# Two MLPs of a vision block: the up-products in five passes of 128 rows instead of six of 96

## The reference, cut to what matters

```python
xn2 = layernorm(x, ln2_g, ln2_b)                       # rows of 192 channels
h = gelu(xn2 @ mlp_w1 + mlp_b1, approximate=False)     # 192 -> 768
x = x + (h @ mlp_w2 + mlp_b2)                          # 768 -> 192
```

## Time and profile before

| | us |
|---|---|
| median of three runs | 1113.1 (1109.18 to 1114.78) |
| the profiled execution | 1113.89, span of its core 1112.1 |
| PE / DVE / ACT / POOL busy | 1031.7 / 848.8 / 700.5 / 169.4 |
| TensorE clock granted, mean | 0.958 |

### The profile page before, as it was taken

The page is one execution under the profiler, slowest core; times in us unless marked ns, Lnnn a source line. Parts: engine busy times, 40 slices in busy tenths (PEclk is TensorE's granted clock), DMA queues, the critical chain, the costliest instruction groups (busy, mean ns, idle before and its releaser), DMA issues.

```text
span 1112.1 us, 35970 instructions
## 1 busy us (share of the span) xinstructions
PE 1031.7 (93%) x15606; PEld 727.9 (65%) x15606; DVE 848.8 (76%) x1714; ACT 700.5 (63%) x1003; POOL 169.4 (15%) x142
## 2 busy tenths in 40 slices
PE   5876879899999999999999999999989888998998
PEld 3555145665777776677677767676657765775776
DVE  4856968899999999999999999999526765233443
ACT  4666056677777777777777877787865442231554
POOL 4430000910000000000000000000024543001443
PEclk9885579999999999999999999999999999999999
DMA  4698966657474757565656566554400011211110
GB/s 126 163 228 274 245 124 152 108 88 135 81 126 92 115 96 108 96 107 100 104 100 104 105 99 109 95 98 85 80 13 22 24 26 33 66 54 40 41 45 22
DMA packets 83043, 109.17 MB, mean 98 GB/s; under 512 B 14141, under 2 KB 75266, under 8 KB 82693
## 3 DMA queue, kind: packets, MB, share of 16 engines
q1 hardware_dynamic: 82885, 106.87, 48.8%
HBM read 85.40 MB, written 21.44 MB: 96 GB/s over the span
## 4 chain that ended last, share of the span: by engine, by line
PE 70%; DVE 13%; DMA 8%; ACT 4%; issue 3%; POOL 2%; SPq 0%; DVEq 0%; ACTq 0%
PE ps L1044 35%; PE ps L1204 17%; PE ps L1039 15%; DVE mx_p L1499 5%; DVE xh L101 2%; POOL rstd L109 1%; DMA m_d<-mneg 1%; DVE stats L88 1%; DMA rel_d<-stage_lo 1%; PE ps L1057 1%; DVE stage_lo L1468 1%; DMA qv<-m_d 1%; DMA rel<-in_c_rel_w 1%; ACT hid_f L971 1%; PE ps L1150 1%
## 5 line engine op out<-in xcount | busy, mean ns | idle before, releaser
L1499 DVE TENSOR_REDUCE mx_p<-ps 128x1 f32<-128x464 f32 (+1 forms) x1080 | 608.2, 627 | 37.2 <-PE ps L1044 27.5
L921 ACT ACTIVATE prob<-ps 128x768 f32<-128x768 f32 x648 | 495.8, 810 | 188.9 <-PE ps L1044 188.3
L1044 PE MATMUL ps<-kc,qc 112*32 112x464 f16 (+1 forms) x4320 | 462.1, 371 | 8.4 <-issue 4.7
L1044 PE MATMUL ps<-qv,ka 113*32 113x384 f16 x5184 | 405.2, 328 | 11.6 <-DMA qv<-m_d 9.2
L1204 PE MATMUL ps<-prob,v_ext 128*32 128x384 f32 x2592 | 294.6, 487 | 3.9 <-issue 3.4
L1044 PEld LDWEIGHTS ps<-qv,ka 113*32 113x32 f16 x5184 | 213.4, 97 | 88.7 <-issue 31.0
L1044 PEld LDWEIGHTS ps<-kc,qc 112*32 112x32 f16 x4320 | 173.4, 96 | 108.2 <-DVE mx_p L1499 29.4
L1204 PEld LDWEIGHTS ps<-prob,v_ext 128*32 128x32 f32 x2592 | 117.1, 111 | 20.1 <-issue 5.8
L1039 PE MATMUL ps<-w_dn,hid 128*96 128x192 f16 x864 | 76.1, 246 | 8.6 <-DVE hid L1554 6.3
L1039 PEld LDWEIGHTS ps<-w_dn,hid 128*96 128x96 f16 x864 | 71.7, 123 | 14.0 <-DVE hid L1554 7.3
L768 POOL COPY v_ext<-v_all 128x288 f32<-128x288 f32 x12 | 5.0, 426 | 479.7 <-PE ps L1204 479.6
(11 more groups left out here) (106 smaller groups left out, 837.2 us busy)
## 6 DMA issues: line engine op xcount, KB each, us to landing
qv<-rel_d SPq DMA_DIRECT2D x216, 144.0 KB
qv<-kq_d SPq DMA_DIRECT2D x108, 216.0 KB
qc<-rel_d SPq DMA_DIRECT2D x24, 216.0 KB, 4.0
xin<-in_x SPq DMA_DIRECT2D x12, 288.0 KB, 3.6
kq_d<-khl SPq DMA_DIRECT2D x24, 144.0 KB, 2.8
q_h<-kq_d SPq DMA_DIRECT2D x9, 288.0 KB, 4.7
q_w<-qw_d SPq DMA_DIRECT2D x9, 288.0 KB, 6.8
rel_d<-stage_hi SPq DMA_DIRECT2D x4, 648.0 KB, 10.1
```

Source lines behind the costliest of these rows:

```text
L921: nc.scalar.activation(prob[:, s4(p, s), :].rearrange("p (a b) -> p a b", a=2), ps[:, 3 + 2 * (s % 2):5 + 2 * (s % 2), 0:CW], ACT.Exp).the ...
L1044: ins = nc.tensor.matmul(ps[c:c + 32, bank, 0:w], l[:, c:c + 32], r, start=True, stop=True, tile_position=(0, c))
L1499: nc.vector.tensor_reduce(mx_p[:, q * GT + k // MP, k % MP:k % MP + 1], ps[:, slot, 0:min(MW, N - k % MP * MW)], AX, ALU.max).then_inc(uni ...
```

## The change

The 192 channels are laid out as 128 and 64. The first part has its high and low halves each on 128 partitions (`x[:, 0]`, `x[:, 1]`). The second part has its high half on partitions 0 to 63 and its low half on 64 to 127 of one plane (`x[:, 2]`), and its weight rows are loaded twice, on both halves of the partitions. One matmul with such a plane does hi x w and lo x w together, so a tile takes 5 matmuls of 128 rows: three for the first part, two for the second (which now takes lo x lo along). `hi_products` has two of them, `lo_products` three. The transposes are still 8, four 128 wide and four 64 wide. ACT makes the two float16 copies by two instructions, DVE the low halves by two. Each MLP's up-weights come by three transfers instead of one, gain and shift by two instead of one.

```diff
-            load(eng, gain[1][:, :], d["L0_conv_ln2_g"].rearrange("(k p) -> p k", p=C2))
-            load(eng, shift[1][:, :], d["L0_conv_ln2_b"].rearrange("(k p) -> p k", p=C2))
-            load(eng, gain[2][:, :], d["L1_conv_g2"].rearrange("(k p) -> p k", p=C2))
-            load(eng, shift[2][:, :], d["L1_conv_be2"].rearrange("(k p) -> p k", p=C2))
+            for dst, nm in ((gain[1], "L0_conv_ln2_g"), (shift[1], "L0_conv_ln2_b"),
+                            (gain[2], "L1_conv_g2"), (shift[2], "L1_conv_be2")):
+                load(eng, dst[:, 0:1], d[nm][0:128].rearrange("(p o) -> p o", o=1))
+                load(eng, dst[0:C - 128, 1:2], d[nm][128:C].rearrange("(p o) -> p o", o=1))
...
-                sp.dma_start(w_up_f[i][:, :, :], d[up].rearrange("(k p) n -> p k n", p=C2)).then_inc(w_mlp_in, 16)
+                sp.dma_start(w_up_f[i][:, 0, :], d[up][0:128, :]).then_inc(w_mlp_in, 16)
+                for r in (0, C - 128):
+                    sp.dma_start(w_up_f[i][r:r + C - 128, 1, :], d[up][128:C, :]).then_inc(w_mlp_in, 16)
...
-                nc.scalar.activation(chunk_of(xnt_all, c)[:, :, 0, :], xnt_f[:, :, :], ACT.Copy).then_inc(x_hi, 1)
+                nc.scalar.activation(x[:, 0, :], xnt_f[:, 0, :], ACT.Copy)
+                nc.scalar.activation(x[0:C - 128, 2, :], xnt_f[0:C - 128, 1, :], ACT.Copy).then_inc(x_hi, 1)
...
-                transposes(xh2[0], bank).then_inc(done, 1)
+                for k, m in enumerate((128, C - 128)):
+                    for t in range(CT):
+                        ins = nc.tensor.transpose(ps[0:m, bank + k, t * T:(t + 1) * T],
+                                                  xh2[0][:, t, k * 128:k * 128 + m], ident[0:T, 0:T])
+                ins.then_inc(done, 1)
...
-                    for k in range(2):
-                        for part in range(2):
-                            mm(ps[:, m % 2, 0:CW], w_up[i][:, k, part, m * 128:(m + 1) * 128], x[:, k, 0, :],
-                               start=(k == 0 and part == 0), stop=False)
+                    w, o = w_up[i][:, :, :, m * 128:(m + 1) * 128], ps[:, m % 2, 0:CW]
+                    mm(o, w[:, 0, 0, :], x[:, 0, :], stop=False)
+                    mm(o, w[:, 0, 1, :], x[:, 0, :], start=False, stop=False)
...
-                    for k in range(2):
-                        ins = mm(ps[:, m % 2, 0:CW], w_up[i][:, k, 0, m * 128:(m + 1) * 128], x[:, k, 1, :],
-                                 start=False, stop=(k == 1))
+                    w, o = w_up[i][:, :, :, m * 128:(m + 1) * 128], ps[:, m % 2, 0:CW]
+                    mm(o, w[:, 0, 0, :], x[:, 1, :], start=False, stop=False)
+                    mm(o, w[:, 1, 1, :], x[:, 2, :], start=False, stop=False)
+                    ins = mm(o, w[:, 1, 0, :], x[:, 2, :], start=False)
...
-                nc.vector.tensor_tensor(x[:, :, 1, :], xnt_f[:, :, :], x[:, :, 0, :], ALU.subtract).then_inc(x_lo, 1)
+                nc.vector.tensor_tensor(x[:, 1, :], xnt_f[:, 0, :], x[:, 0, :], ALU.subtract)
+                nc.vector.tensor_tensor(x[C - 128:128, 2, :], xnt_f[0:C - 128, 1, :], x[0:C - 128, 2, :],
+                                        ALU.subtract).then_inc(x_lo, 1)
```

More of the change, by code:

```diff
@@ L138, in build @@
         w_proj = sb("w_proj", [C2 + 1, 2, C])
-        w_up = [sb("w_up0", [C2, 2, 2, HID], F16)]
+        w_up = [sb("w_up0", [128, 2, 2, HID], F16)]
         w_dn = [sb("w_dn0", [128, 2, HM, C], F16)]
         b_up = [sb(f"b_up{i}", [128, HM]) for i in range(2)]
-        gain = [sb(f"gain{i}", [C2, 2]) for i in range(3)]
-        shift = [sb(f"shift{i}", [C2, 2]) for i in range(3)]
+        gain = [sb(f"gain{i}", [128 if i else C2, 2]) for i in range(3)]
+        shift = [sb(f"shift{i}", [128 if i else C2, 2]) for i in range(3)]
         rows = sb("rows", [T, 4, C])
@@ L180, in build @@
             x1 = sb("x1", [T, NT, C], F32, r)
-            xnt_all = sb("xnt_all", [C2, NC, 2, 2, CW], F16, r)
+            xnt_all = sb("xnt_all", [128, NC, 3, CW], F16, r)
             r3 = sb("r3", [T, NT, C], F32, r)
@@ L198, in build @@
             o_sb = sb("o_sb", [128, 2, CW], F32, r)
-            w_up_f = [sb(f"w_up_f{i}", [C2, 2, HID], F32, r) for i in range(2)]
+            w_up_f = [sb(f"w_up_f{i}", [128, 2, HID], F32, r) for i in range(2)]
             w_dn_f = [sb(f"w_dn_f{i}", [128, HM, C], F32, r) for i in range(2)]
@@ L212, in build @@
         u_sb = sb("u_sb", [4 * KF, CT, C])
-        w_up.append(sb("w_up1", [C2, 2, 2, HID], F16))
+        w_up.append(sb("w_up1", [128, 2, 2, HID], F16))
         w_dn.append(sb("w_dn1", [128, 2, HM, C], F16))
-        xnt_f = sb("xnt_f", [C2, 2, CW])
+        xnt_f = sb("xnt_f", [128, 2, CW])
         y_sb = sb("y_sb", [T, CT, C])
@@ L363, in wait_consts @@
             eng.wait_ge(consts, ALL_CONSTS)
-        ALL_CONSTS = 16 * (2 + 4 + 2 + 4 + 3 + 1 + 2 + 2 * NB)
+        ALL_CONSTS = 16 * (2 + 8 + 2 + 4 + 3 + 1 + 2 + 2 * NB)
         assert GU * 6 == 2 * GS * 5
@@ L389, in chunk_of @@
         def chunk_of(x, c):
-            return x[:, ds(c, 1), :, :, :].rearrange("p o k l t -> p (o k) l t")
+            return x[:, ds(c, 1), :, :].rearrange("p o k t -> p (o k) t")
         def is_at(n, head):
@@ L772, in _ @@
             copy_v(1, 1)
-            pool.wait_ge(w_mlp_in, 64)
+            pool.wait_ge(w_mlp_in, 128)
             for w in w_up_f + w_dn_f:
@@ L907, in norm_transposed @@
                 wait_used(act, x_lo, c + i * NC)
-                for k in range(2):
-                    nc.scalar.activation(xnt_f[:, k, :], ps[0:C2, bank + k, 0:CW], ACT.Identity,
-                                         bias=shift[1 + i][:, k:k + 1], scale=gain[1 + i][:, k:k + 1])\
+                x = chunk_of(xnt_all, c)
+                for k, m in enumerate((128, C - 128)):
+                    nc.scalar.activation(xnt_f[0:m, k, :], ps[0:m, bank + k, 0:CW], ACT.Identity,
+                                         bias=shift[1 + i][0:m, k:k + 1], scale=gain[1 + i][0:m, k:k + 1])\
                       .then_inc(done, 1)
                 act.wait_ge(done, 2 * c + 2)
-                nc.scalar.activation(chunk_of(xnt_all, c)[:, :, 0, :], xnt_f[:, :, :], ACT.Copy).then_inc(x_hi, 1)
+                nc.scalar.activation(x[:, 0, :], xnt_f[:, 0, :], ACT.Copy)
+                nc.scalar.activation(x[0:C - 128, 2, :], xnt_f[0:C - 128, 1, :], ACT.Copy).then_inc(x_hi, 1)
             def period(n, p):
```

1 line of the change is left out of this document (removed).

## The result

The changed kernel takes 1119.4 us (median of 11 runs, 1112.5 to 1125.4) against 1111.9 us (11 runs beside them, 1108.5 to 1117.2): a ratio of 1.0069, 95% interval 1.0047 to 1.0091. Forecast was 1114.1 with a range to 1118.5 and "no change" at 0.83; the time lies above the range, and the kernel is slower. 0.69% of 1111.9 us is 7.7 us.

What follows compares the result with a forecast made beforehand. VectorE's loop bounds the first MLP; up-products partly bound the second, TensorE and ScalarE balanced. Second MLP -2.4, first +1.2, attention +2.2: +1.0 on 1113.9 is 1114.9, that execution 0.8 above median, so 1114.1; range 1109.0 to 1118.5 us.

Steps and rivals of the forecast that it cites:

- no change: Whole kernel: the time cannot be told from that of before, within about 0.5% or 5.6 us; chance 0.83.
- Part 1: Both MLPs: five up-products per tile instead of six, 11.7 us less TensorE work, only some of it reaching the chain.
- TensorE is hidden by VectorE's loop: First MLP, chunks 1 to 5: only earlier Gelus and POOL work help, 0.6 us gained, between 0 and 0.8.
- Part 3: Loads on SP's queue: eight instead of four in head 1 delay `qv`, 1.6 us lost; doubled rows in head 0, 0.5 lost.
- the first rival: Attention: TensorE's stalls grow and its clock drops after the stop in head 1, 1117.3 us; chance 0.22.
- Part 2: Input conversion in two instructions: VectorE's pair without overlap, 0.43 us a chunk (upper bound), 2.1 us lost in the first MLP.
- Second MLP, chunks 1 to 4: Gelu of tile 2 comes 0.49 us earlier per chunk, then ScalarE at 0.97 us a tile limits; 2.0 us gained.
- Last chunk and chunk 0 of the second MLP: Second MLP: last chunk gains 0.65 us from four products fewer; chunk 0 loses 0.2 us waiting for lower halves.
- the doubled rows in head 0: Attention, head 0: two more weight transfers per MLP lengthen TensorE's stops, 0.5 us lost, between -0.5 and 2.
- The lower halves of the second MLP's input: Second MLP: ready at 1038.42, needed at 1038.47, so just hidden; 0.2 us late would cost four chunks 0.8 us.
- TensorE bounds both MLPs: Rival, both MLPs: all 72 saved products count, giving 1101.4 us; chance 0.04.
- the delay on SP's queue is hidden: Rival, head 1: later `qv` costs nothing, and with overlapping halves the time is 1110.9 to 1112.5 us; chance 0.22.

Runs made afterwards that it cites:

- e7: Kernel before with only one up-product per tile left out, five instead of six: 1114.1 us, ratio 1.0034 to the kernel before.
- e1: Changed kernel plus throwaway matmuls on TensorE in the first MLP, ahead of its wait for VectorE's halves: 1116.7 us, ratio 1.0049 to the kernel before.
- e5: Kernel before with only the gain and shift loads in head 1 made eight instead of four: 1113.3 us, ratio 1.0024 to the kernel before.
- e2: Changed kernel with the eight gain and shift loads moved from head 1 to heads 3 to 6: 1113.7 us, ratio 1.0024 to the kernel before.
- e6: Kernel before with only the two-part input conversion, on 96 partitions each: 1115.6 us, ratio 1.0039 to the kernel before.
- e11: Changed kernel with more throwaway matmuls in the first MLP and all small loads moved out of head 1: 1111.6 us, ratio 0.9987 to the kernel before.
- e9: Kernel before with the new layout in the second MLP only, throwaway matmuls in the first, head 1's small loads in heads 3 to 9: 1107.6 us, ratio 0.9964.
- e4: Changed kernel with each tile's first up-product done twice, so six products again: 1122.4 us, ratio 1.0089 to the kernel before.
- e3: Changed kernel with throwaway matmuls in the first MLP and the eight loads moved to heads 3 to 6: 1113.7 us, ratio 1.0008 to the kernel before.
- e8: Kernel before with the new layout in the second MLP only, gain and shift loads in heads 3 to 5: 1109.7 us, ratio 0.9986 to the kernel before.

## Why the prediction was wrong, point by point

- **The step that failed: Part 1, first MLP, chunks 1 to 5, "TensorE is hidden by VectorE's loop".** True of its work, but the saving was given only a gain (0.6 us, "between 0 and 0.8"), and no price for longer stops. The e7 profile shows that the saving alone costs 5.4 us there (117.2 instead of 111.8), and over runs e7, which is that saving and nothing else, is 3.8 us slower where the terms of Part 1 add up to 3.35 us gained: the stop of 1.38 us grew to 3.33, and a hidden engine came out at half its clock. Two things in the step were wrong. The forecast had the loss of clock, but only for attention; the gaps of 1.38 and 2.74 us shown above stood in the profile before, and each tile ahead of them is now a product shorter. And that POOL "works closer together and lets the `h` product" go free sooner had the sign wrong in chunk 1: VectorE's halves came 1.15 us later in e7. Comparing the profile after with e1 puts the price of the clock at 3.7 us; in e7 the two were not separated.
- **Part 3, eight loads: right in mechanism, the size off, forecast +1.6.** Eight loads took 4.64 us of SP's queue, the four before 2.06 (230.52 to 232.58), so `qv` is put off by 2.6. The added wait was 4.83 - 1.24 = 3.6 us, since the landing of `m_d` lengthened as well, and the half-clock stretch came on top, as in the first rival. By e5, which adds them to the kernel before, the whole is 2.7 us over runs, with an interval from 0 to 5.4. The 5 us of e2 are the price of all eight loads, the four old ones with them. The rival had a chance of 0.22 and 1117.3 us, against 1119.4.
- **Part 2, conversion in parts: forecast +2.1, and the first MLP +1.2 in all.** Alone, in e6, it cost 4.3 us over runs (2.3 to 6.3) and 2.1 us of the first MLP in the profile, a half-clock stretch of 3.4 us included. Together with the saving it is 3.1 us beside the clock (e11 against e9), and for another reason than I gave. The pair ran without overlap, 0.57 us apart, near my upper bound, and in chunks 3 and 4, where nothing collides, the period rose by 0.1 us each instead of 0.28 (0.43 less the 0.15 of Part 1). The rest I read as work that moved into POOL's way, and the saving moves it there as well as the conversion. In chunk 0 the root on POOL took 1.73 us, starting 0.17 us behind VectorE's hidden halves, where it took 1.35 us and started 0.08 us behind before. That is the saving's doing: e7 has 1.74 us there, e6 and e4 have 1.35 and 1.36. In chunk 1 the `h` product (0.95 in the earlier trace rows) took 1.68 beside POOL's half of tile 3:

```profile
825.92 1.02 DVE L1564 TENSOR_TENSOR hid<-hid_f,hid 128x384 f16<-128x384 f32 x2
826.09 1.73 POOL L109 TENSOR_TENSOR rstd<-rstd 96x4 f32<-96x4 f32 x1 [0.21 <-DVE rstd L96]
...
841.46 0.91 POOL L797 TENSOR_TENSOR hid<-hid_f,hid 128x384 f16<-128x384 f32 x1 [1.39 <-ACT hid L969]
841.50 1.68 DVE L1584 TENSOR_TENSOR h<-h,rows 96x768 f32<-96x768 f32 x1
```

  In chunk 1 each part alone delays VectorE's halves, the conversion by 0.55 us (e6), the saving by 1.15 (e7), both together by 0.73 (after). The collisions with POOL were not tested by themselves.
- **Second MLP, chunks 1 to 4: -0.49 forecast, -0.27 measured** (14.06 us instead of 14.33). The gain named was there in full: from first up-product to the Gelu of tile 2 it is 1045.62 - 1041.68 = 3.94 us after and 1042.16 - 1037.73 = 4.43 before, 0.49 less (the forecast's 3.8 and 4.3 were both read 0.1 too low). ScalarE's tile is 0.89 us, not 0.97: the 0.97 of before was TensorE's pace, which I read as ScalarE's own; so more was gained behind tile 2, and the down-products begin 6.83 us after the first up-product, not 7.51. Of these 0.68 us, 0.4 are lost on POOL, whose root now starts 0.03 us behind VectorE's pair and takes 1.40 us, where before it started 0.06 us ahead and took 1.01. (e7, whose conversion is undivided, has the same root and 14.05 us too, so it is not the two parts; e4, with six products, has 1.01 to 1.02 us and 14.35.) After, then before:

```profile
1045.62 0.58 ACT L975 ACTIVATE hid_f<-ps,b_up 128x384 f32<-128x384 f32 x1 [1.07 <-PE ps L1043]
1046.51 0.57 ACT L975 ACTIVATE hid_f<-ps,b_up 128x384 f32<-128x384 f32 x1
...
1049.29 1.03 DVE L1564 TENSOR_TENSOR hid<-hid_f,hid 128x384 f16<-128x384 f32 x2 [1.61 <-ACT hid L969]
1049.32 1.40 POOL L109 TENSOR_TENSOR rstd<-rstd 96x4 f32<-96x4 f32 x1
1050.75 1.24 DVE L101 TENSOR_SCALAR xh<-x,mv,rstd 96x192 f32<-96x192 f32 x4 [0.44 <-POOL rstd L109]
```

```profile
1046.05 1.01 POOL L109 TENSOR_TENSOR rstd<-rstd 96x4 f32<-96x4 f32 x1
1046.11 1.03 DVE L1554 TENSOR_TENSOR hid<-hid_f,hid 128x384 f16<-128x384 f32 x2 [1.95 <-ACT hid L965]
```

- **Last chunk and chunk 0 of the second MLP.** From `y_sb` to `y_sb` the last chunk took 11.50 instead of 12.70 us. 0.37 of that is only where the counting starts: behind the divided conversion `y_sb` begins 0.61 us after the first up-product (1098.53 - 1097.92), before it was 0.24 (1095.31 - 1095.07). From the first up-product to the down-products it is 5.96 instead of 6.79 us, 0.83 gained against 0.65 forecast. The stretch that ends with chunk 0 lost 1.15, or 0.78 without that shift, instead of 0.2: the term was too small, and which wait makes it was not tested.
- **Right:** 128 rows cost what 96 do (ten products in 1.79 us after, (1.79 - 0.33) / 9 = 0.162 us each); the doubled rows in head 0 cost nothing that can be seen: the two stops there were 1.17 and 1.85 us after, 2.71 and 3.09 before. Between kernels that are alike in that stretch the first one moved as much: 1.44 to 4.13 us without doubled rows at that place, under 1 to 2.71 with them. Its cause stays open. The lower halves of the second MLP's input were just hidden, as worked out: ten up-products follow each other in 1.79 us.
- **The rivals.** "TensorE bounds both MLPs" is out by e7, "the delay on SP's queue is hidden" by e5's stop. Of the first one, the stop and the half-clock stretch in head 1 came, the longer stops in head 0 did not, and what it said of attention alone happened in the first MLP too. As forecast, a term was taken for every instruction removed or added; what was missing was a term for the time that stays empty.

## What to carry to other kernels

Before work is taken off an engine that is hidden, list its stops in that stretch, make each longer by what is saved, and ask beside what the work behind it will then run: here the clock fell in the longer stops, VectorE's instructions beside POOL's took longer, and the "free" saving made the hidden engine the bound (e7). Throwaway work in the stops turned a part of that back (e1). Change the layout only in the stretch where the trace shows that engine's products on the chain; here half of the change, with the waits of the other half filled and the small loads spread, was faster than both kernels (e9), though its runs do not say how much of that is the layout. When an edit takes something out to price it, count what it takes out beyond the change: e2 took out eight loads where four were new. A pace at which instructions follow each other is not the cost of one, until you have seen who releases them.

## What the runs showed of the hardware

- In the first MLP TensorE's clock was at 1.2 GHz for 3.4 us beside stops of 0.73 us (e5), 0.97, 2.29 and 3.09 (e4), 1.08 (e3), 1.31 and 2.84 (e7), 1.38 and 2.75 (e8) and 2.09 (e6), for 6.8 us beside 3.27 and 4.54 (after), 3.28 and 4.54 (e2) and 3.33 (e7), and not at all beside 1.38 and 2.74 (before), 2.75 (e6) and two of 1.63 (after). What decides between alike stops stays open.
- A start a tenth of a microsecond later, beside VectorE's pair, went with a root on POOL of 1.40 us instead of 1.01, while VectorE's pair stayed at 1.02 to 1.03 us.
- `m_d`, one small row, was down 7.04 us after its issue behind the `qv` transfers, 4.28 us with four loads fewer ahead of them (before), 1.17 us with the loads moved (e2).
- Stops of 2.6 to 3.2 us that the profile names "issue" turned up in head 1 of e2 and e8, where the waits for `m_d` were gone. Their cause was not found.
